# Sobel filter of one pair on GpSimd, rolls by DMA and a shorter divergence in the first half of a four-block image kernel

## The reference

```
g  = relu(bn(dwconv(h, wg)));  g1 = relu(bn(dwconv(h, wg1)))     # depthwise 3x3
gy, gx = sobel(h)                                                # reflecting border
Dx = 1/(gy*gy/4 + 1);  Dy = 1/(gx*gx/4 + 1)
ux = 0.5*(roll(g, 1, 2) - roll(g, -1, 2)); vy = 0.5*(roll(g1, 1, 3) - roll(g1, -1, 3))
E  = (ux + vy)*DT;  D = 1/(1 + 2*Dx*DT + 2*Dy*DT)
for _ in range(5):
    h, h0 = D*(c0*h0 - 2*E*h + cm_x*roll(h,1,2) + cp_x*roll(h,-1,2)
               + cm_y*roll(h,1,3) + cp_y*roll(h,-1,3)) + D*2*DT*fsrc, h
```

## Time and profile before

| | |
|---|---|
| median of 3 runs | 932.79 us (930.93 to 933.65) |
| the profiled execution | 931.59 us, span 929.6 us |
| PE, DVE busy | 749.5 us (81%), 817.1 us (88%) |
| ACT, POOL busy | 552.2 us (59%), 518.2 us (56%) |
| mean granted TensorE clock | 0.969 |
| chain that ended last | DVE 16%, issue 10%, POOL 6%, PE 6%, ACT 5% of the span |
| issue to landing of SP's transfers (medians by line) | 1.9 to 4.0 us |

### The profile page before, as it was taken

How to read it: one execution, slowest core, us unless ns; L and a number is a source line. 1 busy time by engine, 2 the same in 40 slices (tenths; PEclk the granted TensorE clock), 3 DMA queues, 4 the chain that set the end, 5 groups by cost and what they waited for, 6 DMA issues and landing times. The chain is left out here.

```text
span 929.6 us, 10674 instructions
## 1 busy us (share of the span) xinstructions
PE 749.5 (81%) x3902; PEld 499.1 (54%) x3902; DVE 817.1 (88%) x707; ACT 552.2 (59%) x957; POOL 518.2 (56%) x245
## 2 busy tenths in 40 slices
PE   4999997968677688688799899978766677868895
PEld 2444443434366578577655444334436566767873
DVE  6899886779999998999979978767989999899983
ACT  3664233136759898878477433223483978887922
POOL 3005997020479697778410199901136979877841
PEclk9999999999899999999899999989998999999998
DMA  3000000000635455345200200000033445545421
GB/s 110 1 0 0 0 0 0 1 1 0 187 105 185 147 183 181 135 162 194 55 1 0 69 0 0 0 0 1 0 102 114 161 170 185 187 136 182 170 80 23
DMA packets 33296, 75.03 MB, mean 81 GB/s; under 512 B 15708, under 2 KB 15844, under 8 KB 33248
## 3 DMA queue, kind: packets, MB, share of 16 engines
q1 hardware_dynamic: 31840, 73.09, 23.3%
q0 software_dynamic: 320, 1.05, 0.5%
q10 hardware_dynamic: 1088, 0.26, 0.1%
HBM read 70.71 MB, written 2.62 MB: 79 GB/s over the span
## 5 line engine op out<-in xcount | busy, mean ns | idle before, releaser
L389 POOL TENSOR_TENSOR arena<-arena 128x1024 f32<-128x1024 f32 x85 | 202.2, 2389 | 48.1 <-DVE arena L1767 45.0
L961 ACT ACTIVATE arena<-arena 128x128 f32<-128x128 f32 (+3 forms) x408 | 152.5, 448 | 91.9 <-DVE arena L1668 75.3
L1767 DVE TENSOR_TENSOR_SCAN arena<-arena,ps 128x1024 f32<-128x1024 f32 x86 | 194.9, 2278 | 9.7 <-ACT arena L961 7.4
L961 ACT ACTIVATE arena<-arena,Amat 128x1024 f32<-128x1024 f32 x128 | 143.7, 1141 | 8.7 <-DVE arena L1767 7.5
L647 PE MATMUL ps<-mat,arena 128*128 128x128 f32 x1016 | 134.5, 276 | 3.9 <-POOL arena L389 3.4
L606 PE MATMUL ps<-mat,arena 128*128 128x128 f32 x560 | 77.3, 283 | 71.4 <-DVE arena L1767 35.0
L961 ACT ACTIVATE arena<-ps 128x1024 f32<-128x1024 f32 (+2 forms) x65 | 56.1, 873 | 114.3 <-PE ps L480 50.4
L647 PEld LDWEIGHTS ps<-mat,arena 128*128 128x128 f32 x1016 | 116.6, 143 | 7.3 <-POOL arena L389 5.3
L389 POOL TENSOR_TENSOR arena<-HS,arena 128x1024 f32<-128x1024 f32 x42 | 99.5, 2370 | 36.6 <-DVE HS L1767 34.5
L606 PEld LDWEIGHTS ps<-mat,arena 128*128 128x128 f32 x560 | 61.4, 139 | 88.9 <-DVE arena L1767 45.3
L766 PE MATMUL ps<-arena,mat 128*128 128x512 f32 x240 | 106.3, 592 | 0.0
(11 more groups left out here) (218 smaller groups left out, 1389.6 us busy)
## 6 DMA issues: line engine op xcount, KB each, us to landing
arena<-c_rows SPq DMA_DIRECT2D x128, 512.0 KB, 3.8
out<-arena SPq DMA_DIRECT2D x28, 64.0 KB, 2.3
xres<-x POOLq DMA_DIRECT2D x4, 256.0 KB, 5.2
xres<-x SPq DMA_DIRECT2D x4, 256.0 KB, 4.0
arena<-arena SPq DMA_DIRECT2D x4, 252.0 KB
convw<-conv_w SPq DMA_DIRECT2D x1, 576.0 KB
c_rows<-ROWS SPq DMA_DIRECT2D x4, 128.0 KB, 1.9
mat<-mats SPq DMA_DIRECT2D x1, 448.0 KB, 3.6
```

What stands on the lines that cost most here:

```text
L389: tt(HC[s % 2], HS[s % 3], CB[s % 4], ALU.mult).then_inc(S("hc"), 1)
L961: return nc.scalar.activation(out_, in_, func, bias=bias, scale=scale, accum_out=accum_out)
L1767: nc.vector.tensor_tensor_scan(HS[s % 3], DA[s % 3], PS[q][:, :], 0.0, ALU.mult, ALU.add).then_inc(S("scan"), 1)
```

## The change

In half 0 alone, unless half 1 is named:

- The second pair's Sobel filter moves from VectorE to GpSimd (`sobel_second_pair`), in six two-operand instructions (pair sums instead of a multiply-add), with scratch in the second pair's arena.
- The first pair's rolls are done by SP's transfers, as half 1 does them; `rolls(0, 0)` leaves TensorE, and ACT's two copies become two semaphore increments behind the wait for the transfers.
- In both halves the divergence's difference along the width is made by GpSimd (`row_difference`, into `fr`), and TensorE adds it with one matmul per half picture in place of four on parts of rows.
- ACT makes both Sobel frames before the second `first_tap`, the loop state `hw` later (`inner`), and has a new order of `squares`, `relu`, `reciprocal`, `from_D`, `wrap`; `relu(0, 1, 1)` stands behind the first pair's `seed`.
- VectorE has a new order: `sobel(0, 0)` ahead of the second taps, `denominator(0, 0)` ahead of the second pair's taps, `y_neighbours(0, 0)` behind `denominator(0, 1)`, `minus_E(0, 1)` ahead of `times_D(0, 1, 1)`.

The counts of the semaphores `a_sobel`, `a_Sc`, `a_rollm`, `a_rollp` and `rolled` follow. The core of the diff:

```diff
@@ SP
+            roll_first_pair(0)
             for h in range(HALVES):
                 store_rows(h, 0)
@@ GpSimd
+            def sobel_second_pair():
+                a = A[1]
+                fr, sob = frm(a["fr"]), S("a1_sob")
...
+                pool.wait_ge(S("a1_fri"), 4)
+                tt(pairs, fr[:, :, 0:33], fr[:, :, 1:34], ALU.add).then_inc(sob, 1)
+                tt(Y, fr[:, :, 2:34], fr[:, :, 0:32], ALU.subtract).then_inc(sob, 1)
+                pool.wait_ge(sob, 1)
+                tt(X, pairs[:, :, 0:32], pairs[:, :, 1:33], ALU.add).then_inc(sob, 1)
+                pool.wait_ge(sob, 2)
+                tt(rows, Y[:, 0:33, :], Y[:, 1:34, :], ALU.add).then_inc(sob, 1)
+                pool.wait_ge(sob, 3)
+                tt(img(a["R"]), X[:, 2:34, :], X[:, 0:32, :], ALU.subtract)
+                pool.wait_ge(sob, 4)
+                tt(img(a["XY"]), rows[:, 0:32, :], rows[:, 1:33, :], ALU.add).then_inc(sob, 1)
+
+            def row_difference(h, k):
+                g, d = img(A[k]["g"]), img(A[k]["fr"])
+                pool.wait_ge(S(f"a{k}_gg1"), 2 * h + 2)
...
+                tt(d[:, :, 1:31], g[:, :, 2:32], g[:, :, 0:30], ALU.subtract)
+                tt(d[:, :, 0:1], g[:, :, 1:2], g[:, :, 31:32], ALU.subtract)
+                tt(d[:, :, 31:32], g[:, :, 0:1], g[:, :, 30:31], ALU.subtract).then_inc(S("a_Sc"), 1)
@@ GpSimd's list, behind layer_root and root of the tail
+                if h == 0:
+                    sobel_second_pair()
+                row_difference(h, 0)
+                if h > 0:
+                    row_difference(h, 1)
                 source(h, 0)
                 previous_product(h, 0)
+                if h == 0:
+                    row_difference(h, 1)
                 previous_product(h, 1)
@@ TensorE, divergence
-                pe.wait_ge(S(f"a{k}_gg1"), 2 * h + 2)
+                pe.wait_ge(S(f"a{k}_gg1"), 2 * h + 1)
+                pe.wait_ge(S("a_Sc"), source_count(h, f"g{k}"))
...
                 for n in range(2):
-                    r = slice(HB * n, HB * n + HB)
-                    mm(ps[:, r, :], mt("roll_diff"), img(a["g1"])[:, r, :], start=True, stop=False)
-                    mm(ps[:, r, 0:31], ident, g[:, r, 1:32], start=False, stop=False)
-                    mm(ps[:, r, 31:32], ident, g[:, r, 0:1], start=False, stop=False)
-                    mm(ps[:, r, 1:32], mt("neg_ident"), g[:, r, 0:31], start=False, stop=False)
-                    last = mm(ps[:, r, 0:1], mt("neg_ident"), g[:, r, 31:32], start=False, stop=True)
+                    mm(half(PS[2 * k], n), mt("roll_diff"), half(a["g1"], n), start=True, stop=False)
+                    last = mm(half(PS[2 * k], n), ident, half(a["fr"], n), start=False, stop=True)
                 last.then_inc(S("a_div"), 1)
@@ TensorE's list, half 0
-                    rolls(h, 0)
@@ ACT's list, half 0
             first_tap(0, 0, 0)
+            frames(0, 0)
+            frames(0, 1)
             first_tap(0, 0, 1)
-            frames(0, 0)
+            inner(0, 0)
             zero_framed(0, 1)
...
                 if h == 0:
-                    frames(h, 1)
+                    squares(h, 0)
                     relu(h, 0, 0)
-                    squares(h, 0)
+                    inner(h, 1)
                     reciprocal(h, 0)
                     relu(h, 0, 1)
+                    from_D(h, 0)
                     squares(h, 1)
                     relu(h, 1, 0)
-                    from_D(h, 0)
                     reciprocal(h, 1)
+                    for k in range(2):
+                        wrap(h, k, 0)
...
-                    if h > 0 and k == 0:
-                        act.wait_ge(S("rolled"), 128)
+                    if k == 0:
+                        act.wait_ge(S("rolled"), 128 * h + 128)
                         act.sem_inc(S("a_Q5"), 1)
                         act.sem_inc(S("a_Q6"), 1)
...
                         seed(h, 0)
+                        if h == 0:
+                            relu(h, 1, 1)
                         from_D(h, 1)
                         continue
@@ VectorE's list, half 0
                     taps(h, 0, 0)
+                    sobel(h, 0)
                     taps(h, 0, 1)
-                    sobel(h, 0)
+                    denominator(h, 0)
                     taps(h, 1, 0)
                     taps(h, 1, 1)
-                    denominator(h, 0)
-                    sobel(h, 1)
                     fractions(h, 0)
-                    denominator(h, 1)
                     times_D(h, 0, 0)
-                    y_neighbours(h, 0)
                     times_D(h, 0, 1)
                     x_neighbours(h, 0)
+                    denominator(h, 1)
+                    y_neighbours(h, 0)
                     minus_E(h, 0)
                     fractions(h, 1)
...
                     times_D(h, 1, 0)
                     y_neighbours(h, 1)
+                    products(h, 0, 0)
+                    minus_E(h, 1)
                     times_D(h, 1, 1)
                     x_neighbours(h, 1)
                     last_source(h)
-                    minus_E(h, 1)
-                    products(h, 0, 0)
                     previous(h, 0, 0)
                     products(h, 1, 0)
```

More of the change, by code:

```diff
@@ L102, in fused_blocks @@
         arena_cols = max(sum(n for _, n in stage0), sum(n for _, n in later))
-        A, D = [], []
+        SOBEL_W = sum(n for _, n in stage0[:5])
+        SOBEL_H = sum(n for _, n in stage0[:8])
+        A, D, arena_cells = [], [], []
         for k in range(2):
             arena = sb(f"arena{k}", arena_cols)
+            arena_cells.append(arena)
             for parts, table in [(A, stage0), (D, later)]:
@@ L205, in g_shift, with sobel_done, sobel_step, source_count @@
             return 3 * g_count(h, g)
+        def sobel_done(h, k):
+            return 2 * h + k + (h == 0)
+        def sobel_step(h, k):
+            return 4 * h + (h > 0 and k == 1)
+        def source_count(h, name):
+            return 3 * h + [["g0", "source", "g1"], ["g0", "g1", "source"]][h].index(name) + 1
         def off_pe(h, k, w):
@@ L389, in state_times_c @@
                 tt(HC[s % 2], HS[s % 3], CB[s % 4], ALU.mult).then_inc(S("hc"), 1)
+            def sobel_second_pair():
+                a = A[1]
+                fr, sob = frm(a["fr"]), S("a1_sob")
+                X, Y = [a[n].rearrange("p (h w) -> p h w", w=W) for n in "XY"]
+                pairs = arena_cells[1][:, SOBEL_W:SOBEL_W + (H + 2) * (W + 1)].rearrange("p (h w) -> p h w", w=W + 1)
+                rows = arena_cells[1][:, SOBEL_H:SOBEL_H + (H + 1) * W].rearrange("p (h w) -> p h w", w=W)
+                pool.wait_ge(S("a1_fri"), 4)
[12 more added lines that the diff above has]
+                pool.wait_ge(S(f"a{k}_gg1"), 2 * h + 2)
+                if h == 0 and k == 1:
+                    pool.wait_ge(S("a1_sob"), 5)
+                else:
+                    pool.wait_ge(S("a_sobel"), sobel_done(h, k))
+                tt(d[:, :, 1:31], g[:, :, 2:32], g[:, :, 0:30], ALU.subtract)
+                tt(d[:, :, 0:1], g[:, :, 1:2], g[:, :, 31:32], ALU.subtract)
+                tt(d[:, :, 31:32], g[:, :, 0:1], g[:, :, 30:31], ALU.subtract).then_inc(S("a_Sc"), 1)
             def source(h, k):
@@ L525, in divergence @@
                     pe.wait_ge(S("ot"), 2 * h)
-                g, ps = img(a["g"]), img(PS[2 * k])
                 for n in range(2):
-                    r = slice(HB * n, HB * n + HB)
-                    mm(ps[:, r, :], mt("roll_diff"), img(a["g1"])[:, r, :], start=True, stop=False)
-                    mm(ps[:, r, 0:31], ident, g[:, r, 1:32], start=False, stop=False)
-                    mm(ps[:, r, 31:32], ident, g[:, r, 0:1], start=False, stop=False)
-                    mm(ps[:, r, 1:32], mt("neg_ident"), g[:, r, 0:31], start=False, stop=False)
-                    last = mm(ps[:, r, 0:1], mt("neg_ident"), g[:, r, 31:32], start=False, stop=True)
+                    mm(half(PS[2 * k], n), mt("roll_diff"), half(a["g1"], n), start=True, stop=False)
+                    last = mm(half(PS[2 * k], n), ident, half(a["fr"], n), start=False, stop=True)
                 last.then_inc(S("a_div"), 1)
@@ L985, in frames, with inner @@
                 av(fr[:, 33:34, :], fr[:, 31:32, :], ACT.Identity).then_inc(S(f"a{k}_fri"), 1)
+                if h > 0:
+                    inner(h, k)
+            def inner(h, k):
+                a = A[k]
                 gnorm(a, wrapped(a["hw"])[:, :, 1:33], img(xres[k]), h, 0, k).then_inc(S(f"a{k}_h"), 1)
@@ L1003, in squares @@
                 a = A[k]
-                act.wait_ge(S("a_sobel"), 2 * h + k + 1)
+                if h == 0 and k == 1:
+                    act.wait_ge(S("a1_sob"), 5)
+                else:
+                    act.wait_ge(S("a_sobel"), sobel_done(h, k))
                 av(a["Dc"][:, 0:L], a["R"][:, 0:L], ACT.Square, 0.5).then_inc(S(f"a{k}_sq"), 1)
@@ L1046, in seed @@
                 if k == 0:
```

(22 more changed lines are left out.)

## The result

The changed kernel takes 952.53 us (median of 4 runs, 951.08 to 954.03) against 932.13 us of the kernel before in the same series (930.93 to 933.65, 4 runs): ratio 1.0218, with a 95% interval of 1.0195 to 1.0241. It is 20.4 us slower; 953.4 had been forecast. The profiled execution took 952.66 us, with a span of 950.8.

What follows compares the result with a forecast made beforehand. VectorE and TensorE were both taken as full in the preparation, so waits are paid. Shifts of the first `new_h`, 13.7 (first half) + 6.9 (second) = 20.6 us, on median 932.79 gave 953.4; own range 948 to 958, overall 938 to 958.

Steps and rivals of the forecast that it cites:

- The likeliest case: Whole kernel: the forecast itself, 953.4 us with its own range of 948 to 958; chance 0.68.
- 2: First half: GpSimd's filter and VectorE's `sobel(0,0)` take turns from 27.1, so `sobel(0,0)` ends at 41.1 us, without turns 31.8.
- 3: First half: `taps(0,0,1)` stand behind `sobel(0,0)`, TensorE waits 6 us, its third tile ends at 66.2 us (before: 58.3).
- 5: First half: `denominator(0,1)` meets GpSimd's `source(0,0)` and `previous_product(0,0)`; `y_neighbours(0,0)` ends at 75.1 us, without turns 73.5.
- 6: First half: SP's roll takes 9.25 us from release to `field(0)`; `relu(0,1,1)` waits behind `seed(0,0)` and ends at 87.4.
- 7: First half: `row_difference(0,1)` ends at 90.3, `divergence(0,1)` takes 3.5 + 1.9 to 95.8, `x_neighbours(0,1)` ends at 100.6.
- 8: First half: `previous_product(0,1)` 3.06 and three loop products 6.76 put the first `new_h(0,0)` at 110.6, 14.7 later.
- first half: First half: later first `new_h`, and the loop at GpSimd's pace takes 60.8 instead of 61.8 us; +13.7 in all.
- second half: Second half: the first `new_h` +6.9 later, through TensorE's wait for `row_difference(1,0)`, a late `fractions_D(1,1)` and meetings with GpSimd.
- Turns at the ports: VectorE instructions reading two SBUF operands and GpSimd instructions exclude one another and alternate; at the filter, `sobel(0,0)` ends 41.1 instead of 31.8.
- The ports don't block: Rival: VectorE and GpSimd don't hold each other up, `sobel(0,0)` ends at 31.8; +7.6, 940.4 us; chance 0.17.
- Not slower: Rival: without blocking, the VectorE work taken off arrives if `divergence(0,1)` is early enough; -0.9, 931.9 us; chance 0.08.

Runs made afterwards that it cites:

- experiment 2: Changed kernel with GpSimd's filter for the second pair waiting until VectorE's `sobel(0,0)` is done: 948.56 us, ratio 1.0192.
- experiment 3: Changed kernel with `relu(0,1,1)` on ACT put ahead of the wait for the rolled fields: 949.22 us, ratio 1.0185.
- experiment 5: Changed kernel with `relu(0,1,1)` ahead of the roll's wait and the old divergence for the first half's second pair alone: 946.12 us, ratio 1.0146.
- Experiment 1: Changed kernel with the second half alone back to the old divergence, without row differences on GpSimd: 946.45 us, ratio 1.0162.
- experiment 9: experiment 7's kernel with GpSimd's last three filter instructions held until `denominator(0,0)` has read its SBUF pairs, and `minus_E(0,1)` ahead of `products(0,0,0)`: 927.62 us, ratio 0.9948.
- experiment 4: Changed kernel with `minus_E(0,1)` on VectorE put behind `x_neighbours(0,1)` and `last_source(0)`: 950.51 us, ratio 1.0199.
- experiment 7: Changed kernel with GpSimd's filter late, new divergence only for the very first pair, new orders on VectorE and ACT, `source(0,0)` held: 934.90 us, ratio 1.0026.
- experiment 6: Changed kernel with 26 extra matmuls into an unused PSUM bank in TensorE's gap ahead of `divergence(0,1)`: 951.84 us, ratio 1.0208.
- experiment 8: experiment 7's kernel without the hold on GpSimd's `source(0,0)`: 936.89 us, ratio 1.0051.

## Why the prediction was right

The likeliest case came, and by its own steps; the total is off by 0.9 us. That it is so close is in part luck, since errors of up to 1.2 us in single steps cancel. The steps against the trace (forecast, measured):

| step | forecast | measured |
|---|---|---|
| 2: `sobel(0,0)` ends | 41.1 | 40.4 |
| 3: third tile ends | 66.2 | 65.8 |
| 5: `y_neighbours(0,0)` ends | 75.1 | 73.9 |
| 6: release of the roll to `field(0)` | 9.25 us | 9.89 us |
| 6: `relu(0,1,1)` ends | 87.4 | 86.9 |
| 7: row difference | 2.7 us | 2.28 us |
| 7: `divergence(0,1)` | 5.4 us | 6.28 us |
| 8: `new_h(0,0)` | 110.6 | 110.48 |
| first half | +13.7 | +14.0 |
| second half: divergence | 5.4 us | 5.4 us |
| second half: `fractions_D(1,1)` late by | 3.8 | 3.25 |
| second half | +6.9 | +6.2 |

- **Turns at the ports (2, 5).** Shown by experiment 2: VectorE's six instructions need 8.0 us with GpSimd's filter away and 15.6 with it. *The ports don't block* had a chance of 0.17, on the ground of one row, the `pow` of the earlier trace rows. That `pow` lets a VectorE instruction with two SBUF operands through in the changed kernel as well (L1641 takes 1.25 us inside it); every meeting of such an instruction with GpSimd's work on images and weights blocked, in every run here. The blocking started at 24.9, not at 27.1, because L461 met VectorE's filter as well; this and the shorter GpSimd instructions nearly cancel.
- **The roll's chain (6, 7).** Experiments 3 and 5 show that the relu waits behind the roll, as forecast: moved ahead, it starts 5.3 and 5.9 us sooner. The mis-sized terms of this chain are the roll (+0.6) and the clock behind the long gap (2.8 for 1.9), against 0.4 from the row difference and 1.2 from `y_neighbours(0,0)`, of which one instruction alone met GpSimd (1.89 us). Their sum is near nothing, so the 0.1 us at `new_h(0,0)` is luck.
- **The second half.** Experiment 1 takes the whole loss away with the row differences. Of the 6.2, `fractions_D(1,1)` accounts for 3.25 (it starts at 531.61, less 14.02 is 517.59, against 514.34); of the remaining 2.95, two later meetings in that stretch account for 2.7 (1.90 and 3.22 us instead of 1.2). The two parts of the forecast (3.8 and 3.1) were both near, by terms that I didn't separate further.
- **Not slower** took it that nothing blocks, and had its point of decision at the roll. With the relu free of the roll (experiment 5) `new_h(0,0)` is still 6.9 us later than before: GpSimd's meetings have to go as well. Only where most of them do (experiment 9) does `new_h(0,0)` come sooner than before, by 5.9, and there with a roll by transfers.

What stays open: of the 5.9 us that experiment 9 wins at `new_h(0,0)`, 4.1 are left at the second half's first `new_h` (539.35 against 543.44). Between the loops 12 TensorE passes that took 7.08 us behind a 4.68 us gap in the earlier trace rows take 8.11 there behind the same gap, which is 1.0 of it; the rest stays open.

```profile
156.46 8.11 PE L618 MATMUL ps<-arena,diag 128*128 128x512 f32 x12 [4.68 <-DVE arena L1761]
```

## What to carry to other kernels

In these runs work moved from VectorE to GpSimd was free only beside instructions of VectorE that read at most one operand from SBUF; place it by the operands of its neighbours and hold it back with a semaphore where they don't fit. An edit that makes an engine earlier by a few us should be checked for what it then falls upon: experiments 2, 3, 4 and 7 each lost part of their gain that way. And a wait ahead of TensorE can cost more than its length, where the passes behind it run at half clock: look at the granted clock behind each gap, since not every gap here brought it down.

## What the runs showed of the hardware

- The turns are strict for short instructions too: a 32-column GpSimd instruction, 0.29 us alone, takes 1.27 when a VectorE instruction with two SBUF operands is running. VectorE's taps and fractions, with one operand in PSUM, were never stretched, nor did they stretch GpSimd (2.37 us in experiment 9). The Trainium skill (SBUF — State Buffer, Who interferes with whom) states that a VectorE instruction with at most one SBUF input, outside the performance modes that use two ports, does not contend with GpSimd, and that one with two contends with a GpSimd instruction that reads SBUF; these rows agree.
- TensorE's clock fell to 0.50 behind 2.15 us without a matmul (experiment 6), and didn't behind 1.30 (experiment 5). But it didn't behind 3.42 us either (experiment 8), so the length of the gap does not decide alone. The time until it was back at full rate differed from gap to gap: the new divergence, 3.5 us at full rate, lost 3.2 us behind 6.73 us (experiment 3), 2.8 behind 9.86, 2.3 behind 13.96 (experiment 2) and 1.9 behind 6.11, and the same 12 passes behind the same 4.68 us took 7.08 in one kernel and 8.11 in another. A price with bounds, as in the forecast (1.9, between 1.0 and 2.9), is the right form for it; the 3.2 lies outside.
- The time loop has two paces, 6.75 us a step when it starts waiting for GpSimd and 6.87 when it starts waiting for TensorE, and in all runs but that of experiment 9 keeps the one that it began with: a start that is 3 us earlier but changes the pace is worth 2.
